# Two graph layers with layer norms: x turned by DMA, the combination product in f16 halves, and a shifted slot table

## The chip, the cores and the metric

The kernel runs on one core of a Trainium2 chip. The metric is the device time of one execution in microseconds (us). Engines are named as in the profile: PE is TensorE's matmuls, PEld its weight loads, DVE is VectorE, ACT ScalarE, POOL GpSimd, SP the engine that issues nearly all DMAs here.

## The reference

```python
# x: (4096, 256), adj: (4096, 4096) int32 with about 0.2% ones
def layer0(x, adj, ...):
    mask = (adj > 0)
    agg = mask @ x / maximum(sum(mask, axis=1), 1.0)
    combined = concatenate([x @ W_self + b_self, agg @ W_nb + b_nb], axis=-1)
    return relu(combined @ W_comb + b_comb)
def layer1(x, neigh, adj, ...):
    neib_att = tanh(neigh @ Wn1 + bn1) @ Wn2 + bn2
    value = neigh @ Wv + bv
    x_att = tanh(x @ Wx1 + bx1) @ Wx2 + bx2
    ws = leaky_relu(x_att @ neib_att.T, 0.01)
    ws = softmax(where(adj > 0, ws, -9e15), axis=1)
    return concatenate([x @ Wfx + bfx, ws @ value], axis=1)
x = layernorm(x + layer0(x, adj, ...))
x = layernorm(x + layer1(x, neigh, adj, ...))
```

## The kernel before

The 4096 rows are worked on in 32 blocks of 128 (`NB`), the 4096 columns of `adj` in 8 groups of 512 (`NG`) for PE and in 4 quarters of 1024 (`NQ`) for masks, exponentials and DMAs. A product that must be exact is made of f16 halves: a "hi" half rounded to f16 and a "lo" half with the rest. The two 256x256 weight products of layer 0 (`W_self` and `W_nb`, each times its half of `W_comb`) are made once, in `m_both`, in f32. x is kept as scaled f16 halves in `x16`.

The order on every engine is written out by slots. Slot s does group s - 8b of block b's aggregation, and whatever else is due: `due(s, at, 0)` is true for block b at slot 8b + at. The constants at the top of the file are these offsets. So eight slots are one block period, and in each slot of the steady part PE does, in this order:

- `turn_p`: four transposes of exponentials into `ps_t`, group k of block b at slot 8b + 32 + k (`TURN_AT`). For an even k it waits for `exp_made`, the exponential of that quarter.
- `aggregate`: eight products of 256 or 257 columns, mask times x.
- the extras that are due: `mean_transpose` (the mean and x turned on PE), `combine` (four f32 products of 256 columns with `m_both`), `x1_transpose`, `hidden_and_fx`, `x_attention`.
- `scores` into `ps_s` (`SCORE_AT`), and `weigh_values`, twelve products into `ps_v` (`WEIGH_AT`), which wait for `p_lo_made`.

ACT does in a slot, in this order: `mean_of`, the copy of the turned mean and x, `normalise1`, `x1_high`, `x_tanh`, `xatt_high`, `exps` (one quarter of a block, in every second slot, from `ROW_MAX_AT` + 1 on), `p_high`, `leaky`, `normalise2`. DVE does `layer1`, `masked_scores`, `x1_low`, `tanh_low`, `row_scale`, `row_max`, `degrees`, `layer0`, `xatt_low` and `add_fx`, `make_mask`, `p_low`. Each engine runs its list strictly in order; semaphores tie the lists together. Two ties matter below. `mean_of` on ACT waits for `degrees` on DVE of the same slot:

```python
def mean_of(b):
    act.wait_ge(degree_step, 2 * (b + 1))
```

and `turn_p` on PE waits for `exps` on ACT of the slot before:

```python
def turn_p(b, k):
    if k % 2 == 0:
        pe.wait_ge(exp_made, NQ * b + k // 2 + 1)
```

The masks are made on DVE, turned by DMA from SP's queue (`turn_mask`) and followed there by the load of the next block's `adj` quarter.

Of the kernel before, what the change touches and what calls it, by code (L numbers as in the profile page):

```python
# [28 lines left out]
X_ONE, X_LO = D, D + 2  # L29
# [29 lines left out]
X1_T_AT = 15  # L59
X1_COPY_AT = 16  # L60
X1_LOW_AT = 17
HIDDEN_AT = 18
TANH_AT = 19
XATT_AT = 20
STACK_AT = 21
SCORE_AT = 22
# [30 lines left out]
def gnn_kernel(nc, x, adj, w_self, b_self, w_nb, b_nb, w_comb, b_comb, neigh, wx1, bx1, wx2, bx2,  # L97
# [5 lines left out]
    with ExitStack() as ctx:  # L103
# [8 lines left out]
        m_both = sb("m_both", [P, DC, 2 * D], F32)  # L112
# [92 lines left out]
        mask_t_in = [sem(f"mask_t_in{q}") for q in range(NQ)]  # L205
        x_in_in = [sem(f"x_in_in{k}") for k in range(2)]
# [41 lines left out]
        mean_x_t_done = sem("mean_x_t_done")  # L248
# [18 lines left out]
        mean_x_t_copied = sem("mean_x_t_copied")  # L267
# [46 lines left out]
        @block.sync  # L314
        def _(sp):
            def load_adj(b, q):
                at_least(sp, mask_made, NQ * (b - 1) + q + 1)
# [36 lines left out]
            for q in range(NQ):
                turn_mask(0, q)
                load_adj(1, q)
            for s in range(0, SLOTS + 3):
                for q, at in enumerate(MASK_SLOTS):
                    if (d := due(s, at, 0)) and d[0] > 0:
                        turn_mask(d[0], q)  # L360
                        if d[0] + 1 < NB:
# [8 lines left out]

        @block.gpsimd
        def _(pool):
# [57 lines left out]
        def _(dve):  # L430
# [94 lines left out]
            def x1_weight_bounds():  # L525
# [5 lines left out]
            def scale_x1_weights():  # L531
# [3 lines left out]
                scale_link(dve.tensor_scalar(w_scale, w_scale, TOP, None, ALU.mult))  # L535
                scale_link(dve.tensor_scalar(x1_inv, w_pow, 1.0 / TOP / X1_SCALE, None, ALU.mult))
# [58 lines left out]
            def first_part(s):  # L595
# [109 lines left out]
            for s in range(0, SLOTS + 3):  # L705
# [27 lines left out]
        def _(act):  # L733
# [61 lines left out]
            def first_part(s):  # L795
# [73 lines left out]
            for s in range(0, SLOTS + 3):  # L869
# [3 lines left out]
                if d := due(s, MEAN_COPY_AT, 0):  # L873
                    mean_x_t_copy(d[0])
# [19 lines left out]
        def _(pe):  # L894
# [89 lines left out]
            def aggregate(b, k):  # L984
# [142 lines left out]
```

## Time and profile before

| | before |
|---|---|
| time, median of 3 runs | 769.79 us (768.95 to 771.76) |
| profiled execution, its own time | 770.73 us |
| its span, first to last instruction | 768.9 us |
| PE busy | 733.2 us, 95% |
| DVE busy | 610.5 us, 79% |
| ACT busy | 584.7 us, 76% |
| granted TensorE clock | 0.996 of full speed |

Matmuls overlap in these records: the time that one costs is the distance to the next one's start, not its own duration. In the same way an ACT or DVE instruction that needs nothing from its predecessor starts before the predecessor's record ends.

### The profile page before, as it was taken

How to read it: one execution, taken by the hardware profiler on the slowest of the kernel's cores; microseconds unless marked ns; L12 is line 12 of the kernel's file. 1: busy time of each engine (PE TensorE's matmuls, PEld its weight loads, DVE VectorE, ACT ScalarE, POOL GpSimd, SP SyncE). 2: the span in 40 equal slices, each digit the busy share in tenths (PEclk: the TensorE clock that was granted, in tenths of full speed). 3: DMA queues.
4: the chain of work that ended last, by engine and by line, in shares of the span. 5: the costliest groups of instructions: out<-in, count | busy, mean ns of one | idle time of the engine just before them, and what ended most of it. 6: DMA issues, size and time to landing. Idle time of an engine off the chain costs nothing.

```text
span 768.9 us, 20264 instructions
## 1 busy us (share of the span) xinstructions
PE 733.2 (95%) x7536; PEld 631.0 (82%) x7536; DVE 610.5 (79%) x1563; ACT 584.7 (76%) x1078; POOL 125.3 (16%) x241
## 2 busy tenths in 40 slices
PE   5989989999999999999999999999999999999785
PEld 4646768888888888888888889888888888887564
DVE  4886477888888888888888888888888888877874
ACT  2455258888888888888888888888888888888995
POOL 0010120111111111111111111111111111111101
PEclk9999999999999999999999999999999999999999
DMA  8968997876677776676876668677667677620000
GB/s 266 363 151 163 220 246 172 179 173 148 157 150 175 176 180 158 158 156 161 180 179 150 160 164 159 167 180 172 138 171 163 170 179 174 122 43 8 8 9 14
DMA packets 175154, 120.43 MB, mean 157 GB/s; under 512 B 140368, under 2 KB 158672, under 8 KB 175056
## 3 DMA queue, kind: packets, MB, share of 16 engines
q1 hardware_dynamic: 174612, 119.11, 65.1%
q8 instruction: 60, 0.98, 0.6%
q14 instruction: 38, 0.31, 0.1%
q10 hardware_dynamic: 444, 0.02, 0.0%
HBM read 81.35 MB, written 4.19 MB: 111 GB/s over the span
## 4 chain that ended last, share of the span: by engine, by line
PE 87%; ACT 4%; DVE 3%; issue 3%; DMA 1%; POOL 1%; SPq 0%; POOLq 0%; ACTq 0%; DVEq 0%
PE ps_v L1036 20%; PE ps_t L1023 14%; PE ps_agg L999 14%; PE ps_agg L1002 14%; PE ps_agg L1056 7%; PE ps_s L1014 6%; PE ps_v L921 2%; PE ps_s L913 2%; PE ps_x L1073 1%; PE ps_x L1076 1%; ACT score L829 1%; DMA neigh_sb<-in_L_gnn_neigh_dram 1%; ACT score L822 1%; PE ps_x L930 1%; PE ps_t L904 1%
## 5 line engine op out<-in xcount | busy, mean ns | idle before, releaser
L999 PE MATMUL ps_agg<-x,mask_t 128*128 128x257 f16 x1024 | 239.7, 272 | 1.5 <-DMA mask_t<-mask 1.5
L1002 PE MATMUL ps_agg<-x,mask_t 128*128 128x256 f16 x1024 | 234.5, 272 | 0.0
L679 DVE TENSOR_TENSOR late<-ps_t,late 128x512 f16<-128x512 f32 x256 | 174.8, 683 | 74.2 <-ACT late L835 71.6
L1036 PEld LDWEIGHTS ps_v<-v,late 128*128 128x128 f16 x3072 | 189.9, 97 | 50.9 <-DVE late L679 16.6
L1036 PE MATMUL ps_v<-v,late 128*128 128x128 f16 x3072 | 213.5, 219 | 9.2 <-DVE late L679 6.7
L822 ACT ACTIVATE score<-ps_s,sc 128x512 f32<-128x512 f32 x256 | 178.0, 695 | 53.0 <-PE ps_s L1014 51.5
L622 DVE CUSTOM_DVE_ANT_0 score<-score,mask 128x512 f32<-128x512 f32 x256 | 176.2, 688 | 18.7 <-ACT score L822 17.2
L835 ACT CAST late<-ps_t 128x512 f16<-128x512 f32 x256 | 150.2, 587 | 15.2 <-PE ps_t L1023 15.1
L1023 PE MATMUL ps_t<-ident,score 128*128 128x128 f32 x1024 | 157.3, 276 | 3.4 <-ACT score L829 3.4
L829 ACT ACTIVATE score<-score,exp_bias,sc 128x1024 f32<-128x1024 f32 x128 | 158.7, 1240 | 1.6 <-DVE exp_bias L631 1.6
L1023 PEld LDWEIGHTS ps_t<-ident,score 128*128 128x128 f32 x1024 | 107.9, 141 | 6.8 <-ACT score L829 4.7
L999 PEld LDWEIGHTS ps_agg<-x,mask_t 128*128 128x128 fp8e4 x1024 | 99.6, 97 | 16.0 <-DMA mask_t<-mask 1.7
L1002 PEld LDWEIGHTS ps_agg<-x,mask_t 128*128 128x128 fp8e4 x1024 | 99.3, 97 | 15.4 <-issue 4.9
L1014 PE MATMUL ps_s<-n,stack 96*128 96x512 f16 x256 | 97.4, 381 | 0.9 <-DVE stack L669 0.9
L486 DVE TENSOR_SCALAR mask<-adj_sb 128x1024 bf16<-128x1024 int32 x128 | 89.6, 702 | 1.1 <-issue 0.2
L415 POOL TENSOR_SCALAR mv<-mv 128x1 f32<-128x1 f32 x32 | 18.9, 591 | 255.5 <-DVE mv L703 255.5
L1056 PE MATMUL ps_agg<-m_both,mean_x_t 128*128 128x256 f32 x256 | 60.5, 379 | 0.0
L812 ACT ACTIVATE mean<-ps_agg,row 128x256 f32<-128x256 f32 x32 | 15.1, 473 | 49.5 <-DVE row L640 49.5
L401 POOL TENSOR_SCALAR mv<-mv 128x1 f32<-128x1 f32 x32 | 8.4, 262 | 261.8 <-DVE mv L653 261.8
L1056 PEld LDWEIGHTS ps_agg<-m_both,mean_x_t 128*128 128x128 f32 x256 | 46.1, 190 | 5.3
L410 POOL TENSOR_TENSOR late<-x,bfv_sb 128x256 f32<-128x256 f32 x32 | 23.8, 745 | 54.2 <-ACT x L841 54.2
L1014 PEld LDWEIGHTS ps_s<-n,stack 96*128 96x128 f16 x256 | 25.0, 98 | 2.9 <-DVE stack L669 1.1
(125 smaller groups left out, 705.7 us busy)
## 6 DMA issues: line engine op xcount, KB each, us to landing
adj_sb<-in_adj_dram SPq DMA_DIRECT2D x128, 512.0 KB, 4.7
neigh_sb<-in_L_gnn_neigh_dram SPq DMA_DIRECT2D x8, 512.0 KB, 8.0
score<-in_x_dram SPq DMA_DIRECT2D x8, 512.0 KB, 8.5
x_in<-in_x_dram SPq DMA_DIRECT2D x32, 128.0 KB, 3.9
out_dram<-out_sb SPq DMA_DIRECT2D x32, 128.0 KB, 4.5
mask_t<-mask SPq DMA_TRANSPOSE x128, 4.2
mask<-in_L_gnn_W_comb_dram SPq DMA_DIRECT2D x1, 512.0 KB, 10.1
mask<-in_L_gnn_W_self_dram SPq DMA_DIRECT2D x1, 256.0 KB, 7.1
```

The costliest lines, as they stand in the source:

```text
L486: dve.tensor_scalar(mask[:, b % MASK_BUFS, q * QW:(q + 1) * QW], adj_sb[:, q, :], 0.0, EDGE, ALU.is_le, ALU.add).then_inc(mask_made, 1)
L622: dve.tensor_tensor_reduce(score[:, b % 2, part], score[:, b % 2, part], mask[:, b % MASK_BUFS, part], 1.0, -3.0e38, ALU.subtract, ALU.max ...
L679: dve.tensor_tensor(p_lo[:, k % 2, :], ps_t[k % 2][:, :], p_hi[:, k % 2, :], ALU.subtract).then_inc(p_lo_made, 1)
L822: act.activation(score[:, b % 2, k * GW:(k + 1) * GW], ps_s[k % 2][:, :], ACT.Prelu, alpha=SLOPE, scale=score_scale).then_inc(leaky_made, 1)
L829: act.activation(part, part, ACT.Exp, bias=exp_bias[:, b % 2:b % 2 + 1], scale=score_unit, accum_out=sums[:, b % 2, q:q + 1]).then_inc(exp ...
L835: act.copy(p_hi[:, k % 2, :], ps_t[k % 2][:, :]).then_inc(p_hi_made, 1)
L999: mm = pe.matmul(agg[:, 0:D + 1], mask_t8[:, c, 0, :], x16[:, c, 0:D + 1], start=(c == 0), stop=(c == NC - 1), skip_group_check=True)
L1002: mm = pe.matmul(agg[:, 0:D], mask_t8[:, c, 0, :], x16[:, c, X_LO:X_LO + D], start=False, stop=False, skip_group_check=True)
L1014: pe.matmul(ps_s[k % 2][:, :], stack[:, b % 2, :], n16[:, k * GW:(k + 1) * GW], start=True, stop=True).then_inc(s_done, 1)
L1023: mm = pe.transpose(ps_t[k % 2][:, u * P:(u + 1) * P], score[:, b % 2, at:at + P], ident[:, :])
L1036: mm = pe.matmul(ps_v[:, 0:DV], p[:, k % 2, chunk], v16[:, c, v:v + DV], start=(c == 0 and part == 0), stop=(c == NC - 1 and part == 2))
L1056: mm = pe.matmul(ps_agg[b % 2][:, 0:D], mean_x_t[:, c * P:(c + 1) * P], m_both[:, dc, half * D:(half + 1) * D], start=(c == 0), stop=(c == ...
```

## The change

x is no longer turned on PE. For each block SP issues one DMA transpose of `x16[:, b]` (both f16 halves, 128x512) into `x_t`. The turned mean is split into f16 halves (`mean_t`), the hi half by ACT (`mean_high`), the lo half by DVE (`mean_low`). `m_both` is scaled and split into `m16` once, during the first slots. `combine` is now twelve f16 products of 256 columns: hi-hi, hi-lo and lo-hi, each over two chunks, for x and for the mean. The result is scaled back in `layer0`'s first operation (`l0_inv`).

```diff
-MASK_SLOTS = (-6, -5, -2, -1)
+MASK_SLOTS = (-7, -5, -1, 0)
 MEAN_AT = 8
 MEAN_T_AT = 9
-MEAN_COPY_AT = 10
-COMBINE_AT = 11
-LAYER0_AT = 12
-X1_AT = 14
+MEAN_SPLIT_AT = 10
+MEAN_LOW_AT = 11
+X_TURN_AT = 4
+COMBINE_AT = 12
+LAYER0_AT = 13
+X1_AT = 15
...
-ROW_MAX_AT = 30
-TURN_AT = 32
-WEIGH_AT = 33
-LAYER1_AT = 41
+ROW_MAX_AT = 31
+TURN_AT = 33
+WEIGH_AT = 34
+LAYER1_AT = 42
...
+            def turn_x(b):
+                sp.wait_ge(x_lo_made, b // TR + 1)
+                at_least(sp, combined, b - 1)
+                sp.dma_start_transpose(x_t[:, b % 2, :, :], x16[:, b, 0:2 * D]).then_inc(x_t_in[b % 2], 16)
...
+            def m_low(c):
+                dve.wait_ge(m_hi_made, c + 1)
+                dve.scalar_tensor_tensor(out=m16[:, 1, c, :], in0=m_both[:, c, :], scalar=m_scale, in1=m16[:, 0, c, :],
+                                         op0=ALU.mult, op1=ALU.subtract).then_inc(m_split, 1)
...
+            def mean_low(b):
+                dve.wait_ge(mean_hi_made, b + 1)
+                dve.scalar_tensor_tensor(out=mean_t[:, 1, :], in0=ps_agg[b % 2][:, 0:D], scalar=x_scale,
+                                         in1=mean_t[:, 0, :], op0=ALU.mult, op1=ALU.subtract).then_inc(mean_lo_made, 1)
...
-            def mean_x_t_copy(b):
-                act.wait_ge(mean_x_t_done, b + 1)
+            def mean_high(b):
+                act.wait_ge(mean_t_done, b + 1)
                 at_least(act, combined, b)
-                act.copy(mean_x_t[:, :], ps_agg[b % 2][:, :]).then_inc(mean_x_t_copied, 1)
+                act.activation(mean_t[:, 0, :], ps_agg[b % 2][:, 0:D], ACT.Copy, scale=x_scale).then_inc(mean_hi_made, 1)
...
             def mean_transpose(b):
                 pe.wait_ge(mean_made, b + 1)
-                pe.wait_ge(x_in_in[b % 2], 16 * (b // 2 + 1))
                 for dc in range(DC):
-                    pe.transpose(ps_agg[b % 2][:, dc * P:(dc + 1) * P], mean[:, dc * P:(dc + 1) * P], ident[:, :])
-                for dc in range(DC):
-                    mm = pe.transpose(ps_agg[b % 2][:, D + dc * P:D + (dc + 1) * P],
-                                      x_in[:, b % 2, dc * P:(dc + 1) * P], ident[:, :])
-                mm.then_inc(mean_x_t_done, 1)
+                    mm = pe.transpose(ps_agg[b % 2][:, dc * P:(dc + 1) * P], mean[:, dc * P:(dc + 1) * P], ident[:, :])
+                mm.then_inc(mean_t_done, 1)
 
             def combine(b):
-                pe.wait_ge(mean_x_t_copied, b + 1)
-                for c in range(2 * DC):
-                    half, dc = divmod(c, DC)
-                    mm = pe.matmul(ps_agg[b % 2][:, 0:D], mean_x_t[:, c * P:(c + 1) * P],
-                                   m_both[:, dc, half * D:(half + 1) * D], start=(c == 0), stop=(c == 2 * DC - 1))
+                if b == 0:
+                    pe.wait_ge(m_split, DC)
+                pe.wait_ge(x_t_in[b % 2], 16 * (b // 2 + 1))
+                pe.wait_ge(mean_lo_made, b + 1)
+                for k, ((r, w), dc) in enumerate(product(HI_LO, range(DC))):
+                    pe.matmul(ps_agg[b % 2][:, 0:D], x_t[:, b % 2, (1 - r) * DC + dc, :], m16[:, w, dc, D:2 * D],
+                              start=(k == 0), stop=False)
+                for k, ((r, w), dc) in enumerate(product(HI_LO, range(DC))):
+                    mm = pe.matmul(ps_agg[b % 2][:, 0:D], mean_t[:, r, dc * P:(dc + 1) * P], m16[:, w, dc, 0:D],
+                                   start=False, stop=(k == 3 * DC - 1))
                 mm.then_inc(combined, 1)
```

All constants between `X1_AT` and `LAYER1_AT` grow by one, so that everything from `combine` on stands one slot later against the aggregation, and the program has one slot more. `MEAN_AT` and `MEAN_T_AT` stay.

On PE, around `combine`, there stood before (`L1056` is `combine`, `L1014` `scores`, `L1036` `weigh_values`, `L1023` `turn_p`, the others `aggregate`):

```order
L999 MATMUL ps_agg<-x,mask_t 128x257
L1056 MATMUL ps_agg<-m_both,mean_x_t 128x256 x4
L1014 MATMUL ps_s<-n,stack 128x512
L1036 MATMUL ps_v<-v,late 128x128 x12
L1023 MATMUL ps_t<-ident,score 128x128 x4
```

and now (`L1097` and `L1100` are `combine`, `L1057` `scores`, `L1079` `weigh_values`, `L1066` `turn_p`):

```order
L1042 MATMUL ps_agg<-x,mask_t 128x257
L1097 MATMUL ps_agg<-m,x_t 128x256 x6
L1100 MATMUL ps_agg<-m,mean_t 128x256 x6
L1057 MATMUL ps_s<-n,stack 128x512
L1079 MATMUL ps_v<-v,late 128x128 x12
L1066 MATMUL ps_t<-ident,score 128x128 x4
```

Four f32 products have become twelve f16 ones; the place within the slot is the same.

On ACT, from the slot 7 places into the block period to the one after it wraps, there stood before (`L841` is `normalise1`, `L835` `p_high`, `L822` `leaky`, `L829` `exps`, `L812` `mean_of`, `L853` `x1_high`):

```order
L841 ACTIVATE x<-l,mv 128x256
L835 CAST late<-ps_t 128x512
L822 ACTIVATE score<-ps_s,sc 128x512
L829 ACTIVATE score,sums<-score,exp_bias,sc 128x1024
L835 CAST late<-ps_t 128x512
L822 ACTIVATE score<-ps_s,sc 128x512
L812 ACTIVATE mean<-ps_agg,row 128x256
L853 ACTIVATE x_t<-ps_x 128x256
L835 CAST late<-ps_t 128x512
L822 ACTIVATE score<-ps_s,sc 128x512
L829 ACTIVATE score,sums<-score,exp_bias,sc 128x1024
```

and now (`L884` is `normalise1`, `L878` `p_high`, `L865` `leaky`, `L855` `mean_of`, `L872` `exps`, `L896` `x1_high`, `L860` `mean_high`):

```order
L884 ACTIVATE x<-l,mv 128x256
L878 CAST late<-ps_t 128x512
L865 ACTIVATE score<-ps_s,sc 128x512
L855 ACTIVATE mean<-ps_agg,row 128x256
L872 ACTIVATE score,sums<-score,exp_bias,sc 128x1024
L878 CAST late<-ps_t 128x512
L865 ACTIVATE score<-ps_s,sc 128x512
L896 ACTIVATE x_t<-ps_x 128x256
L878 CAST late<-ps_t 128x512
L865 ACTIVATE score<-ps_s,sc 128x512
L860 ACTIVATE mean_t<-ps_agg,sc 128x256
```

The first exponential after `normalise1`'s slot now stands behind `mean_of`; before, it stood a slot ahead of it, and `mean_of` had a `p_high` and a `leaky` between itself and the next exponential.

On DVE, at the same place, there stood before (`L622` is `masked_scores`, `L486` `make_mask`, `L679` `p_low`, `L685` to `L689` `row_scale`, `L637` and `L640` `degrees`):

```order
L622 ISA score,part_max<-score,mask 128x512
L622 ISA part_max 128x1
L486 TENSOR_SCALAR mask<-adj_sb 128x1024
L679 TENSOR_TENSOR late<-ps_t,late 128x512
L622 ISA score,part_max<-score,mask 128x512
L622 ISA part_max 128x1
L685 TENSOR_REDUCE row<-sums 128x1
L687 RECIPROCAL row<-row 128x1
L689 TENSOR_SCALAR row<-row,sc 128x1
L637 TENSOR_SCALAR row<-ps_agg,sc 128x1
L640 RECIPROCAL row<-row 128x1
L679 TENSOR_TENSOR late<-ps_t,late 128x512
```

and now (`L659` and `L662` are `row_max`, `L505` `make_mask`, `L717` `p_low`, `L653` `masked_scores`, `L668` and `L671` `degrees`):

```order
L659 TENSOR_REDUCE row<-part_max 128x1
L662 TENSOR_SCALAR exp_bias<-row,sc 128x1
L505 TENSOR_SCALAR mask<-adj_sb 128x1024
L717 TENSOR_TENSOR late<-ps_t,late 128x512
L653 ISA score,part_max<-score,mask 128x512
L653 ISA part_max 128x1
L668 TENSOR_SCALAR row<-ps_agg,sc 128x1
L671 RECIPROCAL row<-row 128x1
L505 TENSOR_SCALAR mask<-adj_sb 128x1024
L717 TENSOR_TENSOR late<-ps_t,late 128x512
```

`row_scale` no longer stands ahead of `degrees`, `row_max` and a mask now stand in the slot before it, and `masked_scores` is still ahead of it.

## Rows read from the trace of the kernel before

**Rows 1.** Windows: first slots, one block period, tail (busy, count, clock, DMA)

```profile
60.00:80.00 20.00, 20.00 (x124) 12.14 (x123) 13.51 (x27) 10.22 (x15) 0.62 (x1) 1.00 0.70 154
400.21:421.10 20.89, 20.89 (x229) 18.67 (x228) 17.48 (x46) 17.13 (x32) 3.75 (x7) 1.00 0.66 165
720.00:740.00 20.00, 16.00 (x183) 12.34 (x183) 16.63 (x49) 18.82 (x36) 2.79 (x5) 1.00 0.02 8
```

**Rows 2.** Waits of PE from 120 to 700 us: the whole answer

```profile
PE ps_t L1023 <- ACT score L829: 0.2, 1, 0.2
```

**Rows 3.** Timeline of PE over one block period: start us, us, instruction

```profile
400.21 0.22 PE L1082 MATMUL ps_x<-tanh,wx 96*96 96x128 f16 x1
...
405.58 0.60 PE L1023 MATMUL ps_t<-ident,score 128*128 128x128 f32 x4
...
408.01 0.61 PE L1023 MATMUL ps_t<-ident,score 128*128 128x128 f32 x4
...
410.22 0.61 PE L1023 MATMUL ps_t<-ident,score 128*128 128x128 f32 x4
...
411.76 0.38 PE L1048 MATMUL ps_agg<-ident,x_in 128*128 128x128 f32 x2
411.98 0.38 PE L1014 MATMUL ps_s<-n,stack 96*128 96x512 f16 x1
412.20 0.83 PE L1036 MATMUL ps_v<-v,late 128*128 128x128 f16 x12
412.92 0.66 PE L1023 MATMUL ps_t<-ident,score 128*128 128x128 f32 x4
413.41 0.27 PE L1002 MATMUL ps_agg<-x,mask_t 128*128 128x256 f16 x1
...
414.29 0.50 PE L1073 MATMUL ps_x<-x_t,wx 128*96 128x128 f16 x6
...
417.17 1.89 PE L1056 MATMUL ps_agg<-m_both,mean_x_t 128*128 128x256 f32 x8
418.89 0.38 PE L1014 MATMUL ps_s<-n,stack 96*128 96x512 f16 x1
...
421.10 0.22 PE L1082 MATMUL ps_x<-tanh,wx 96*96 96x128 f16 x1
```

**Rows 4.** Timeline of ACT around `mean_of`

```profile
405.70 1.23 ACT L829 ACTIVATE score<-score,exp_bias,sc 128x1024 f32<-128x1024 f32 x1
406.83 0.19 ACT L829 ACTIVATION_READ_ACCUMULATOR score<-score,exp_bias,sc 128x1 f32 x1
...
409.83 0.47 ACT L812 ACTIVATE mean<-ps_agg,row 128x256 f32<-128x256 f32 x1 [1.60 <-DVE row L640]
410.21 0.38 ACT L853 ACTIVATE x_t<-ps_x 128x256 f16<-128x256 f32 x1
...
411.51 1.26 ACT L829 ACTIVATE score<-score,exp_bias,sc 128x1024 f32<-128x1024 f32 x1
412.65 0.22 ACT L829 ACTIVATION_READ_ACCUMULATOR score<-score,exp_bias,sc 128x1 f32 x1
```

**Rows 5.** Timeline of DVE around `degrees`

```profile
406.30 0.67 DVE L622 CUSTOM_DVE_ANT_0 score<-score,mask 128x512 f32<-128x512 f32 x1
...
406.90 0.68 DVE L486 TENSOR_SCALAR mask<-adj_sb 128x1024 bf16<-128x1024 int32 x1
...
409.39 0.21 DVE L637 TENSOR_SCALAR row<-ps_agg,sc 128x1 f32<-128x1 f32 x1
409.64 0.16 DVE L640 RECIPROCAL row<-row 128x1 f32<-128x1 f32 x1
```

**Rows 6.** Groups by line, 350 to 518 us: busy us, mean ns

```profile
L657 DVE SCALAR_TENSOR_TENSOR x_t<-ps_x,x_t 128x256 f16<-128x256 f32 x9 | 3.8, 420 | 0.0
L817 ACT COPY mean_x_t<-ps_agg 128x512 f32<-128x512 f32 x9 | 5.6, 617 | 0.0
```

**Rows 7.** DMA issues, 350 to 518 us: median us from issue to landing

```profile
mask_t<-mask SPq DMA_TRANSPOSE x32, 3.8
```

More of the change, by code:

```diff
@@ L28 @@
 XW = 2 * D + 2
-X_ONE, X_LO = D, D + 2
+X_LO, X_HI, X_ONE = 0, D, 2 * D
 EDGE = 1.5 * 2.0 ** -121
@@ L48 @@
 RES_BUFS = 4
-MASK_SLOTS = (-6, -5, -2, -1)
+MASK_SLOTS = (-7, -5, -1, 0)
 MEAN_AT = 8
 MEAN_T_AT = 9
-MEAN_COPY_AT = 10
-COMBINE_AT = 11
-LAYER0_AT = 12
-X1_AT = 14
[L59 to L66, printed above, removed]
-ROW_MAX_AT = 30
-TURN_AT = 32
-WEIGH_AT = 33
-LAYER1_AT = 41
+MEAN_SPLIT_AT = 10
[4 more added lines that the diff above has]
+X1_AT = 15
+X1_T_AT = 16
+X1_COPY_AT = 17
+X1_LOW_AT = 18
+HIDDEN_AT = 19
+TANH_AT = 20
+XATT_AT = 21
+STACK_AT = 22
+SCORE_AT = 23
+ROW_MAX_AT = 31
+TURN_AT = 33
+WEIGH_AT = 34
+LAYER1_AT = 42
 SLOTS = NG * (NB - 1) + LAYER1_AT + 1
@@ L111, in gnn_kernel @@
         neigh_sb = sb("neigh_sb", [P, NB, D], F32)
-        m_both = sb("m_both", [P, DC, 2 * D], F32)
+        m16 = sb("m16", [P, 2, DC, 2 * D], F16)
         v16 = sb("v16", [P, NC, 2 * DV], F16)
@@ L125, in gnn_kernel @@
         bfv_sb = sb("bfv_sb", [P, D], F32)
-        sc = sb("sc", [P, 32], F32)
-        w_top, w_pow, w_scale, x1_inv = sc[:, 24:26], sc[:, 26:28], sc[:, 28:30], sc[:, 30:32]
-        fx_inv, h1_inv = sc[:, 30:31], sc[:, 31:32]
+        sc = sb("sc", [P, 40], F32)
+        w_top, w_pow, w_scale, x1_inv = sc[:, 24:27], sc[:, 27:30], sc[:, 30:33], sc[:, 33:35]
+        m_pow, m_scale, l0_inv = sc[:, 29:30], sc[:, 32:33], sc[:, 35:36]
+        fx_inv, h1_inv = sc[:, 33:34], sc[:, 34:35]
         score_unit, minus_unit, unit_inv = sc[:, 20:21], sc[:, 21:22], sc[:, 22:23]
@@ L146, in gnn_kernel @@
         res = late[:, 1024:2048].rearrange("p (r d) -> p r d", r=RES_BUFS)
+        m_both = late[:, 0:DC * 2 * D].rearrange("p (c d) -> p c d", c=DC)
         x_in = sb("x_in", [P, 2, D], F32)
@@ L149, in gnn_kernel @@
         mean = sb("mean", [P, D], F32)
-        mean_x_t = sb("mean_x_t", [P, 2 * D], F32)
+        mean_t = sb("mean_t", [P, 2, D], F16)
+        x_t = sb("x_t", [P, 2, 2 * DC, P], F16)
         x1 = sb("x1", [P, D], F32)
@@ L205, in gnn_kernel @@
         mask_t_in = [sem(f"mask_t_in{q}") for q in range(NQ)]
+        x_t_in = [sem(f"x_t_in{k}") for k in range(2)]
         x_in_in = [sem(f"x_in_in{k}") for k in range(2)]
@@ L266, in gnn_kernel @@
         mean_made = sem("mean_made")
-        mean_x_t_copied = sem("mean_x_t_copied")
+        mean_hi_made = sem("mean_hi_made")
+        mean_lo_made = sem("mean_lo_made")
+        m_hi_made = sem("m_hi_made")
+        m_split = sem("m_split")
+        m_scaled = sem("m_scaled")
         p_hi_made = sem("p_hi_made")
@@ L362, in _ @@
                             load_adj(d[0] + 1, q)
+                if d := due(s, X_TURN_AT, 0):
+                    turn_x(d[0])
                 if d := due(s, LAYER0_AT + 1, 0):
@@ L475, in x_low @@
                 dve.scalar_tensor_tensor(out=x16[:, part, X_LO:X_LO + D], in0=x_sb[:, part, :], scalar=x_scale,
-                                         in1=x16[:, part, 0:D], op0=ALU.mult, op1=ALU.subtract).then_inc(x_lo_made, 1)
+                                         in1=x16[:, part, X_HI:X_HI + D], op0=ALU.mult, op1=ALU.subtract).then_inc(x_lo_made, 1)
             def make_mask(b, q):
@@ L529, in x1_weight_bounds, with scale_late_weights @@
                                       apply_absolute_value=True).then_inc(w_top_made, 1)
-            def scale_x1_weights():
+                dve.wait_ge(m_copied, DC)
+                dve.tensor_reduce(w_top[:, 2:3], m_both[:, :, :], AX.XY, ALU.max,
+                                  apply_absolute_value=True).then_inc(w_top_made, 1)
+            def scale_late_weights():
                 dve.wait_ge(w_top_reduced, 1)
@@ L534, in scale_x1_weights @@
                 scale_link(dve.reciprocal(w_scale, w_pow))
-                scale_link(dve.tensor_scalar(w_scale, w_scale, TOP, None, ALU.mult))
-                scale_link(dve.tensor_scalar(x1_inv, w_pow, 1.0 / TOP / X1_SCALE, None, ALU.mult))
+                dve.tensor_scalar(w_scale, w_scale, TOP, None, ALU.mult).then_inc(m_scaled, 1)
+                dve.wait_ge(m_scaled, 1)
+                scale_link(dve.tensor_scalar(x1_inv, w_pow[:, 0:2], 1.0 / TOP / X1_SCALE, None, ALU.mult))
+                scale_link(dve.tensor_scalar(l0_inv, x_pow, m_pow, 1.0 / TOP / TOP, ALU.mult, ALU.mult))
             def split_fx():
@@ L606, in first_part @@
                 if s == 3:
-                    x1_weight_bounds()
+                    late_weight_bounds()
                 if s == 5:
-                    scale_x1_weights()
-                if s == 7:
+                    scale_late_weights()
+                if s in (6, 7):
+                    m_low(s - 6)
+                if s == 9:
                     split_fx()
@@ L636, in degrees @@
                 at_least(dve, mean_made, b)
-                dve.tensor_scalar(row[:, 4:5], ps_agg[b % 2][:, X_ONE:X_ONE + 1], EDGE_F8, x_scale, ALU.max,
+                dve.tensor_scalar(row[:, 4:5], ps_agg[b % 2][:, D:D + 1], EDGE_F8, x_scale, ALU.max,
                                   ALU.mult).then_inc(degree_step, 1)
@@ L644, in layer0 @@
                 dve.wait_ge(combined, b + 1)
+                dve.wait_ge(x_in_in[b % 2], 16 * (b // 2 + 1))
                 at_least(dve, x1_made, b)
-                dve.tensor_tensor(l0[:, :], ps_agg[b % 2][:, 0:D], z_bias[:, :], ALU.add).then_inc(l0_step, 1)
+                dve.scalar_tensor_tensor(out=l0[:, :], in0=ps_agg[b % 2][:, 0:D], scalar=l0_inv, in1=z_bias[:, :],
+                                         op0=ALU.mult, op1=ALU.add).then_inc(l0_step, 1)
                 dve.wait_ge(l0_step, base + 1)
@@ L710, in _ @@
                     masked_scores(*d)
+                if d := due(s, MEAN_LOW_AT, 0):
+                    mean_low(d[0])
                 if d := due(s, X1_LOW_AT, 0):
@@ L765, in x_high @@
                 part = slice(TR * i, TR * (i + 1))
-                act.activation(x16[:, part, 0:D], x_sb[:, part, :], ACT.Copy, scale=x_scale).then_inc(x_hi_made, 1)
+                act.activation(x16[:, part, X_HI:X_HI + D], x_sb[:, part, :], ACT.Copy, scale=x_scale).then_inc(x_hi_made, 1)
             act.wait_ge(neigh_w_in, 16 * len(NEIGH_WEIGHTS))
@@ L807, in first_part @@
                     x_high(s + 2)
+                if s in (6, 7):
+                    act.wait_ge(m_scaled, 1)
+                    act.activation(m16[:, 0, s - 6, :], m_both[:, s - 6, :], ACT.Copy, scale=m_scale).then_inc(m_hi_made, 1)
             def mean_of(b):
                 act.wait_ge(degree_step, 2 * (b + 1))
-                at_least(act, mean_x_t_done, b)
+                at_least(act, mean_t_done, b)
                 act.activation(mean[:, :], ps_agg[b % 2][:, 0:D], ACT.Copy, scale=row[:, 5:6]).then_inc(mean_made, 1)
-            def mean_x_t_copy(b):
-                act.wait_ge(mean_x_t_done, b + 1)
+            def mean_high(b):
+                act.wait_ge(mean_t_done, b + 1)
                 at_least(act, combined, b)
-                act.copy(mean_x_t[:, :], ps_agg[b % 2][:, :]).then_inc(mean_x_t_copied, 1)
+                act.activation(mean_t[:, 0, :], ps_agg[b % 2][:, 0:D], ACT.Copy, scale=x_scale).then_inc(mean_hi_made, 1)
             def leaky(b, k):
@@ L872, in _ @@
                     mean_of(d[0])
-                if d := due(s, MEAN_COPY_AT, 0):
-                    mean_x_t_copy(d[0])
+                if d := due(s, MEAN_SPLIT_AT, 0):
+                    mean_high(d[0])
                 if d := due(s, X1_AT, 0):
@@ L998, in aggregate @@
                         if part == "hi":
-                            mm = pe.matmul(agg[:, 0:D + 1], mask_t8[:, c, 0, :], x16[:, c, 0:D + 1], start=(c == 0),
+                            mm = pe.matmul(agg[:, 0:D + 1], mask_t8[:, c, 0, :], x16[:, c, X_HI:X_ONE + 1], start=(c == 0),
                                            stop=(c == NC - 1), skip_group_check=True)
```

8 lines of the change are left out of this document (4 added, 4 removed).

## The prediction

> **What bounds the kernel now.** I read the windows first. In a block period of the steady part PE is busy for all of its 20.89 us, DVE for 17.48, ACT for 17.13, and the DMA engines for 0.66 of it [rows 1]. Then the waits of PE: over 580 us one wait of 0.2 us stands there [rows 2]. So from 120 to 700 us the time is the sum of what PE issues. The tail after the last aggregation is another regime: ACT is busy 18.82 of 20 us there, PE 16.00 [rows 1]. Then the timeline of one period, for the margins behind that full PE. Take the slots modulo 8; I call the slot that starts with `turn_p` at 405.58 slot 7, those at 408.01, 410.22 and 412.92 slots 0, 1 and 2 [rows 3]. A plain slot costs PE 2.21 us (408.01 to 410.22). The exponential that slot 0's `turn_p` needs ends at 406.83 + 0.19 = 407.02 [rows 4], 0.99 us before 408.01 [rows 3]. The one that slot 2's `turn_p` needs ends at 412.65 + 0.22 = 412.87 [rows 4], and the turn starts at 412.92 [rows 3]. The products ahead of it take 2.21 - 0.44 - 0.88 - 0.22 = 0.67 us (0.44 being what a turn takes where PE does not wait, an estimate close to four times 0.11; 8 aggregations 0.88; a score 411.98 to 412.20), so PE was free at 412.87: about 0.05 us of waiting, too short for a row of its own. So this kernel is PE-bound with one place where the margin is nil, and the reader should see what makes it nil: ACT stood idle 1.60 us before `mean_of`, waiting for DVE's `degrees` [rows 4], and DVE reached `degrees` only at 409.39 [rows 5], though the aggregation it reads was complete in slot 7.
>
> **PE's own work.** Removed per block: the f32 products, 417.17 to 418.89, 1.72 us, and x's two transposes, 411.76 to 411.98, 0.22 us [rows 3]. Added: twelve f16 products of 256 columns. Eight of this shape took 413.41 to 414.29, 0.88 us, so 0.11 each [rows 3] and 1.31 for twelve. Net 0.63 us less per block. 31 of 32 combinations stand before the last aggregation, in both versions, and there PE is full: 31 x 0.63 = 19.5 us less. The last one is in the tail, where PE isn't the bound: nothing.
>
> **Small engine work.** ACT's copy of 128x512 (617 ns [rows 6]) becomes one of 128x256, like the 0.38 us of `x1_high` [rows 4]. DVE gains `mean_low`, like the lo half of x1, 420 ns [rows 6]: 17.9 us per period. Both lie under PE. The turned x needs to be there at slot 12 and is asked for at slot 4, eight slots or some 17 us ahead; a mask turn of twice the size lands in 3.8 us [rows 7]. If the cover failed, it would cost at most its landing, under 4 us a block. On SP it stands behind the mask of slot 3 and ahead of the store, and the next mask turn is three slots later. The mask quarters are now made 7, 7, 5 and 6 slots before use instead of 6, 7, 6 and 7: 11 us and more against 3.8. Nothing. The one-time split of `m_both` (a reduce of 128x1024, four operations of 128x512) falls in the first slots, where PE is full for 20 us and DVE works 13.51 of 20 [rows 1]: nothing, with up to 2 us in the range.
>
> By the Trainium skill ("VectorE: DVE Perf Modes", The three transpose paths) a 128x128 transpose takes 1309 ns by DMA and 390 on TensorE, and TensorE is its choice where PSUM will do; here a turn of eight such blocks lands in 3.8 us and two on PE cost 0.22 us, so the trace prices both below the page. By the page's figure the four blocks would take 5.2 us, and if they took all DMA engines, 13.8 + 5.2 = 19.0 of 20.9 us would be filled, near the limit. By the rows it is at most half of 3.8 us, 1.9 us, on top of 0.66 x 20.89 = 13.8 us: 15.7, with room.
>
> **One slot more.** Scores and weighing stand one slot later, so one slot's share of them (2.21 - 0.88 = 1.33 us of PE) leaves the PE-bound part and one slot is added to the tail. There ACT sets the pace (94% busy [rows 1]); its 17.13 us per period are 2.14 a slot, of which I take 2.0, since some small work of the last blocks doesn't come again. Together +0.7 us.
>
> **The new wait.** This decides. `turn_p`, `exps` and `row_max` have moved by a slot, `mean_of` has not. Thus the contents of the old slot 7 now stand in slot 0, together with `degrees` and `mean_of`, and on ACT `mean_of` is directly ahead of the exponential for slot 1's `turn_p`. ACT cannot begin that exponential before DVE has done `degrees`, which is behind `masked_scores`. All the rest up to there (the score, `leaky`, `row_max`, mask, `p_low`, `masked_scores`) is what the old slots 5 to 7 held, in the same order, with the same PE slots beside it, so I put the new instructions into the old slot 7's clock:
>
> - `masked_scores` starts at 406.30, and the next DVE instruction at 406.90 [rows 5]. That is now `degrees`.
> - From the start of `degrees` to that of `mean_of`: 409.39 to 409.83, 0.44 us [rows 4, 5]. `mean_of` at 407.34.
> - `mean_of` to the next ACT instruction: 409.83 to 410.21, 0.38 us [rows 4]. The exponential starts at 407.72, instead of 405.70: 2.02 us late.
> - Exponential to the turn that waits for it: 1.32 us (405.70 to 407.02) to 1.41 (411.51 to 412.92) [rows 3, 4]; 1.39 taken. The turn can start at 409.11.
> - PE is ready for it one slot after 405.58, with `x1_transpose` in it as before: at 408.01 [rows 3].
>
> PE stands still 1.10 us, in every block. Queued behind: the whole of slot 1. No slack of an earlier slot absorbs it, since the chain starts at a score that PE itself issues two slots before. What follows has room: the exponential's 1.23 us from 407.72, then `p_high` (at most the 0.62 of a copy of its size [rows 6]) and `p_low` (taken like the 0.67 of `masked_scores`) end at 410.24, and slot 1's products want them at 409.11 + 0.44 + 0.88 + 0.22 + 0.22 = 410.87, 0.6 us later; in slot 2 the exponential that was just in time before now has no `mean_of` in its chain; its old wait of 0.05 us goes. The combination slot is shorter by 0.42 us, and ACT, which waited in it before, is then just in step.
>
> The wait exists where `mean_of` of block b and the exponential of block b - 3 share a slot: b = 3 to 31, 29 times. 29 x 1.10 = 31.9 us, less 29 x 0.05 = 1.5.
>
> **Sum.** -19.5 + 0.7 + 31.9 - 1.5 = +11.6 us. It is made against the profiled execution (770.73 us, span 768.9), which is 0.9 us above the median of the runs shown, 769.79. On the median: 781.4, say 781.5 us, 1.5% slower.
>
> **Bounds of the wait.** Below: if DVE reached `masked_scores` as soon as `leaky` is done, about 0.5 us earlier than in the old slot 7, the wait would be 0.6 and the sum -3 us. Above: if slot 1 or 2 has a second, smaller wait behind it (the 0.6 us margin for `p_low` used up by clumping on DVE), 0.2 to 0.3 us more a block: +20 us.
>
> **Rivals.**
> - *PE stays full and the kernel is faster.* `mean_of` waits, but the exponential's margin (0.99 us) covers it. It decides if the exponential is less than 1.0 us late instead of 2.02. For it: PE shows no wait now. Against it: the 1.60 us idle before `mean_of` is there already, only with nothing urgent behind. Time: 769.8 - 19.5 - 0.8 = 749.5, or up to 755 with 0.2 us left of the wait.
> - *Gain and wait cancel.* The wait is 0.5 to 0.8 us: 764 to 773.
> - *DMA becomes a bound as well.* The blocks before the scores begin are shorter than 20.9 us and need the same transfers, and every block now adds one. With 0.4 us more a block than my sum: 790 to 797. Against: 15.7 us of DMA in a period of 21.3.
> - *The split's latency.* `mean_high` and `mean_low` don't reach PE by slot 12. They have two slots, some 4 us, for about 0.8 us of work; the time would be as in the case before.
>
> **How the numbers follow.** Forecast (the wait at 0.85 to 1.35 us, 774 to 789) 0.68; PE stays full 0.13; cancel 0.11; DMA or another second wait 0.08. The range takes the forecast, the upper half of the cancelling case and the lower edge of the last: 769 to 791. A measurement can tell this kernel's time to about 0.5%, 3.8 us. Faster: the first rival and a little of the second, 0.15; within 0.5%: 0.10; slower: 0.75.
>
> **What the profile after would show.** Right: PE waits at `turn_p` for ACT's exponential, some 29 times by about 1.1 us, all in slot 1; ACT idles about 1.6 us before `mean_of` with the exponential next; the period is 21.35 us, with the twelve products taking 1.31 in it. PE busy per period falls below it for the first time. Wrong: a period of 20.26 us with PE full (the first rival), waits for `x_t` or `mask_t` (DMA), or for `mean_lo_made`. The prediction fails if DVE runs far enough ahead of its old clock in slot 7, since only there the chain could shrink.

## The result, and the profile after

The changed kernel takes 784.28 us (median of 4 runs, 782.34 to 785.46) against 769.37 us of the kernel before beside it (4 runs, 768.84 to 771.76): ratio 1.0185, 95% interval 1.0155 to 1.0216. It is slower, and the prediction was 781.5.

The profiled execution took 785.46 us with a span of 783.7. First its windows: the first blocks, two short stretches behind them, and one block period (columns as in [rows 1]):

```profile
100.00:113.00 13.00, 10.68 (x91) 8.15 (x90) 10.37 (x30) 7.19 (x15) 1.85 (x3) 1.00 1.17 283
113.00:120.00 7.00, 4.07 (x18) 2.98 (x19) 4.09 (x10) 3.75 (x8) 0.79 (x1) 0.67 0.96 198
116.60:122.20 5.60, 5.60 (x25) 4.39 (x26) 3.03 (x7) 3.26 (x6) 0.00 (x0) 0.50 1.12 276
400.93:422.29 21.36, 20.49 (x233) 18.29 (x230) 17.66 (x48) 17.10 (x34) 3.76 (x8) 1.00 0.77 168
```

The period was 20.89 us with PE full [rows 1]; it is 21.36 with PE busy 20.49. Then the waits of PE from 120 to 700 us, again the whole answer:

```profile
PE ps_t L1066 <- ACT score L872: 23.5, 27, 0.9
```

One wait per block, at `turn_p`, for the exponential: 27 in this window, one before it and one behind it. [rows 2] held 0.2 us. Then PE's timeline around it, slots 7, 0 and 1:

```profile
411.87 0.61 PE L1066 MATMUL ps_t<-ident,score 128*128 128x128 f32 x4
...
414.10 0.61 PE L1066 MATMUL ps_t<-ident,score 128*128 128x128 f32 x4
...
415.87 0.83 PE L1079 MATMUL ps_v<-v,late 128*128 128x128 f16 x12
417.57 0.66 PE L1066 MATMUL ps_t<-ident,score 128*128 128x128 f32 x4 [0.87 <-ACT score L872]
```

The twelve products from 415.87 on need 0.67 us, so PE was free at 416.54 and began at 417.57: 1.03 us. The bracket says 0.87 because matmul records overlap. ACT and DVE over the same stretch (`L855` is `mean_of`, `L872` `exps`, `L653` `masked_scores`, `L668` and `L671` `degrees`, `L717` `p_low`, `L505` `make_mask`):

```profile
406.95 0.69 DVE L717 TENSOR_TENSOR late<-ps_t,late 128x512 f16<-128x512 f32 x1 [1.41 <-ACT late L878]
...
413.49 0.77 DVE L505 TENSOR_SCALAR mask<-adj_sb 128x1024 bf16<-128x1024 int32 x1
414.18 0.68 DVE L717 TENSOR_TENSOR late<-ps_t,late 128x512 f16<-128x512 f32 x1
414.78 0.68 DVE L653 CUSTOM_DVE_ANT_0 score<-score,mask 128x512 f32<-128x512 f32 x1
...
415.38 0.21 DVE L668 TENSOR_SCALAR row<-ps_agg,sc 128x1 f32<-128x1 f32 x1
415.63 0.16 DVE L671 RECIPROCAL row<-row 128x1 f32<-128x1 f32 x1
```

```profile
415.82 0.47 ACT L855 ACTIVATE mean<-ps_agg,row 128x256 f32<-128x256 f32 x1 [1.51 <-DVE row L671]
416.20 1.23 ACT L872 ACTIVATE score<-score,exp_bias,sc 128x1024 f32<-128x1024 f32 x1
417.33 0.19 ACT L872 ACTIVATION_READ_ACCUMULATOR score<-score,exp_bias,sc 128x1 f32 x1
```

Read it from the bottom: the turn at 417.57 waited for the exponential's end at 417.52, the exponential for `mean_of`, `mean_of` for the reciprocal, and that for `masked_scores`. ACT was idle 1.51 us with an exponential behind the instruction that it waited with. In [rows 4] the idle time is nearly the same, 1.60 us, but the exponential had been issued a slot earlier.

Above `masked_scores` the chain goes on along DVE's own queue. `p_low` and a mask stand ahead of it, and DVE had no gap of more than 0.05 us since the `p_low` at 406.95, 7.8 us earlier. So it is DVE's backlog that sets when `degrees` runs, and ACT's order that hands the delay on to PE.

Where the 14.8 us of span come from can be read off the transposes of the mean, one pair per block, which stand in the same slot in both kernels. In the kernel before, those of the first, fifth and last block start at:

```profile
76.44 0.38 PE L1046 MATMUL ps_agg<-ident,mean 128*128 128x128 f32 x2
...
139.99 0.38 PE L1046 MATMUL ps_agg<-ident,mean 128*128 128x128 f32 x2
...
702.80 0.44 PE L1046 MATMUL ps_agg<-ident,mean 128*128 128x128 f32 x2 [0.41 <-ACT mean L812]
```

and in the changed one at:

```profile
75.26 0.38 PE L1088 MATMUL ps_agg<-ident,mean 128*128 128x128 f32 x2
...
141.36 0.38 PE L1088 MATMUL ps_agg<-ident,mean 128*128 128x128 f32 x2
...
716.59 0.38 PE L1088 MATMUL ps_agg<-ident,mean 128*128 128x128 f32 x2
```

So the changed kernel is 1.2 us ahead at the first block and 1.4 us behind at the fifth. It loses 12.4 us in the 27 periods after that (0.46 each), and 1.0 us behind the last mean, where the added slot lies.

### The profile page after: what moved, and what is told of

Its sections match the earlier page's. It is cut to its first block, busy times and chain, and to the rows that moved or that the text cites. A ratio compares the mean times of both kernels' runs of the same rounds, so it can differ in the third digit from the quotient of the medians.

```text
span 783.7 us, 20493 instructions
## 1 busy us (share of the span) xinstructions
PE 723.5 (92%) x7600; PEld 620.5 (79%) x7600; DVE 619.9 (79%) x1599; ACT 584.7 (75%) x1080; POOL 125.2 (16%) x241
## 4 chain that ended last, share of the span: by engine, by line
PE 57%; issue 16%; DVE 12%; ACT 10%; SPq 2%; DMA 1%; POOL 1%; ACTq 0%; POOLq 0%; DVEq 0%
PE ps_v L1079 11%; PE ps_t L1066 10%; PE ps_agg L1042 9%; PE ps_agg L1045 9%; DVE score L653 5%; ACT score L872 5%; PE ps_s L1057 4%; ACT score L865 3%; PE ps_agg L1097 3%; PE ps_agg L1100 3%; PE ps_x L1117 1%; DVE late L717 1%; PE ps_x L1120 1%; SPq L357 1%; PE ps_s L956 1%
## 5 line engine op out<-in xcount | busy, mean ns | idle before, releaser
L717 DVE TENSOR_TENSOR late<-ps_t,late 128x512 f16<-128x512 f32 x256 | 174.7, 682 | 99.7 <-ACT late L878 98.5
L1042 PE MATMUL ps_agg<-x,mask_t 128*128 128x257 f16 x1024 | 244.6, 274 | 0.1
L1045 PE MATMUL ps_agg<-x,mask_t 128*128 128x256 f16 x1024 | 238.7, 274 | 0.3 <-DVE x L494 0.3
L865 ACT ACTIVATE score<-ps_s,sc 128x512 f32<-128x512 f32 x256 | 177.0, 691 | 71.9 <-PE ps_s L1057 71.9
L1079 PEld LDWEIGHTS ps_v<-v,late 128*128 128x128 f16 x3072 | 191.1, 97 | 46.9 <-DVE late L717 16.8
L1079 PE MATMUL ps_v<-v,late 128*128 128x128 f16 x3072 | 213.5, 219 | 9.2 <-DVE late L717 7.0
L1066 PE MATMUL ps_t<-ident,score 128*128 128x128 f32 x1024 | 158.1, 277 | 29.8 <-ACT score L872 29.8
L653 DVE CUSTOM_DVE_ANT_0 score<-score,mask 128x512 f32<-128x512 f32 x256 | 175.5, 686 | 9.6 <-ACT score L865 9.5
L878 ACT CAST late<-ps_t 128x512 f16<-128x512 f32 x256 | 148.5, 580 | 16.0 <-PE ps_t L1066 15.8
L872 ACT ACTIVATE score<-score,exp_bias,sc 128x1024 f32<-128x1024 f32 x128 | 158.0, 1234 | 1.6 <-DVE exp_bias L662 1.6
L1066 PEld LDWEIGHTS ps_t<-ident,score 128*128 128x128 f32 x1024 | 108.5, 141 | 36.4 <-ACT score L872 35.7
L1045 PEld LDWEIGHTS ps_agg<-x,mask_t 128*128 128x128 fp8e4 x1024 | 100.7, 98 | 16.3 <-issue 5.2
L1042 PEld LDWEIGHTS ps_agg<-x,mask_t 128*128 128x128 fp8e4 x1024 | 100.9, 98 | 15.5 <-issue 0.8
L1057 PE MATMUL ps_s<-n,stack 96*128 96x512 f16 x256 | 97.6, 381 | 0.9 <-DVE stack L707 0.9
L505 DVE TENSOR_SCALAR mask<-adj_sb 128x1024 bf16<-128x1024 int32 x128 | 89.5, 702 | 0.3
L855 ACT ACTIVATE mean<-ps_agg,row 128x256 f32<-128x256 f32 x32 | 15.1, 473 | 46.3 <-DVE row L671 46.3
L884 ACT ACTIVATE x<-l,mv 128x256 f32<-128x256 f32 x32 | 19.1, 598 | 11.6 <-POOL mv L424 11.6
L1057 PEld LDWEIGHTS ps_s<-n,stack 96*128 96x128 f16 x256 | 25.0, 98 | 2.7 <-DVE stack L707 1.2
L903 ACT ACTIVATE tanh<-ps_x,bx_sb,sc 96x128 f32<-96x128 f32 x64 | 25.2, 445 | 2.0 <-PE ps_x L1120 2.0
```

The source lines that it names most:

```text
L505: dve.tensor_scalar(mask[:, b % MASK_BUFS, q * QW:(q + 1) * QW], adj_sb[:, q, :], 0.0, EDGE, ALU.is_le, ALU.add).then_inc(mask_made, 1)
L653: dve.tensor_tensor_reduce(score[:, b % 2, part], score[:, b % 2, part], mask[:, b % MASK_BUFS, part], 1.0, -3.0e38, ALU.subtract, ALU.max ...
L717: dve.tensor_tensor(p_lo[:, k % 2, :], ps_t[k % 2][:, :], p_hi[:, k % 2, :], ALU.subtract).then_inc(p_lo_made, 1)
L865: act.activation(score[:, b % 2, k * GW:(k + 1) * GW], ps_s[k % 2][:, :], ACT.Prelu, alpha=SLOPE, scale=score_scale).then_inc(leaky_made, 1)
L872: act.activation(part, part, ACT.Exp, bias=exp_bias[:, b % 2:b % 2 + 1], scale=score_unit, accum_out=sums[:, b % 2, q:q + 1]).then_inc(exp ...
L878: act.copy(p_hi[:, k % 2, :], ps_t[k % 2][:, :]).then_inc(p_hi_made, 1)
```

## The experiments

All times below are medians of 4 or 5 runs. The first four experiments built (`mean_of` last, `degrees` first, the shift alone, the layout alone) ran beside the kernel before at 769.60 us, the other four on another chip beside it at 769.66 us. A period is the mean over the transposes of x1 from the fourth to the thirtieth block.

**mean_of issued last.** On ACT, in the changed kernel:

```diff
-                if d := due(s, MEAN_AT, 0):
-                    mean_of(d[0])
...
                 if d := due(s, SCORE_AT):
                     leaky(*d)
+                if d := due(s, MEAN_AT, 0):
+                    mean_of(d[0])
```

> The changed kernel with one line moved on ACT: mean_of is issued behind leaky of its slot instead of ahead of the exponential. Theory (the wait of TensorE at turn_p is the exponential held up behind mean_of, 1.03 us in each of 29 blocks): the wait goes, the period falls from 21.35 to about 20.35 us, TensorE is full again, time 752 to 757 us. Rival (ACT or DVE are simply overloaded in that slot, or the split and the DMA turn hold TensorE up): the work is the same, so the wait only moves and the time stays within 3 us of 784.

Measured: 750.52 us, ratio 0.9748 (0.9733 to 0.9762). The period in a window, first blocks and one period:

```profile
100.00:125.00 25.00, 21.71 (x201) 17.52 (x199) 20.04 (x55) 17.57 (x34) 2.64 (x4) 1.00 1.14 253
400.00:420.27 20.27, 20.27 (x231) 18.23 (x229) 17.74 (x48) 17.08 (x32) 3.25 (x7) 1.00 0.84 176
```

and ACT at the same place:

```profile
416.29 1.23 ACT L872 ACTIVATE score<-score,exp_bias,sc 128x1024 f32<-128x1024 f32 x1
...
418.72 0.47 ACT L855 ACTIVATE mean<-ps_agg,row 128x256 f32<-128x256 f32 x1
```

PE is full again, the period 1.08 us shorter, and `mean_of` has no wait in front of it at all: the reciprocal that it needs has been done for 0.86 us. DVE's work and its order are the same, so load alone doesn't hold PE up, and the overload rival is out in that form. The time came out 1.5 us below the expected range. The period is 0.08 us shorter than expected, and the first wait fell from 2.83 to 1.14 us, with the granted clock at 1.00 from 100 to 125 us.

**degrees issued first.** On DVE `degrees` is moved ahead of `masked_scores`:

```diff
+                if d := due(s, MEAN_AT, 0):
+                    degrees(d[0])
                 if d := due(s, SCORE_AT + 1):
                     masked_scores(*d)
...
-                if d := due(s, MEAN_AT, 0):
-                    degrees(d[0])
```

> The changed kernel with degrees issued ahead of masked_scores on DVE. Theory (chain p_low, masked_scores, degrees, mean_of, exponential, turn): masked_scores' 0.60 us leave the chain, so the wait shrinks from 1.03 to about 0.43 us and the time by 29 x 0.60 = 17 us to about 767 us. Rival (the slot is overloaded, order does not matter): no change, 784.

Measured: 764.29 us, ratio 0.9926 (0.9912 to 0.9941). The turn in question and its exponential:

```profile
405.48 0.66 PE L1066 MATMUL ps_t<-ident,score 128*128 128x128 f32 x4 [0.26 <-ACT score L872]
```

```profile
403.73 0.47 ACT L855 ACTIVATE mean<-ps_agg,row 128x256 f32<-128x256 f32 x1 [0.90 <-DVE row L671]
404.10 1.23 ACT L872 ACTIVATE score<-score,exp_bias,sc 128x1024 f32<-128x1024 f32 x1
```

ACT's idle time shrank by 0.61 us (1.51 to 0.90) and the period by as much, 21.35 to 20.75. So the wait has the size of the chain: taking 0.6 us out of it gives 0.6 us back. The time is 2.7 us below the expected 767. As with `mean_of` last, the first wait is shorter (1.68 us) and the granted clock stays at 1.00 from 100 to 125 us. By the same reading, the 0.69 us mask in front of `p_low` is another link that could be moved; no run tried that.

**The shift alone.** The kernel before, with `MASK_SLOTS = (-7, -5, -1, 0)` and each of the fifteen constants from `COMBINE_AT` to `LAYER1_AT` one higher:

```diff
-COMBINE_AT = 11
+COMBINE_AT = 12
...
-ROW_MAX_AT = 30
+ROW_MAX_AT = 31
...
-LAYER1_AT = 41
+LAYER1_AT = 42
```

> The kernel before with the shifted slots and the new mask slots alone: f32 combination and transposes of x on TensorE as before. Theory (the shift alone makes the wait, the products alone save): 769.4 + 29 x 1.0 + 0.7 for the slot + 1.5 for the first blocks = about 800 us, a period of about 21.9 us. Rival (the split of the mean or the DMA turn makes the wait): 769 to 772 us.

Measured: 800.11 us, ratio 1.040 (1.038 to 1.042), period 21.92, as expected. Nothing of the split or the DMA turn is in this kernel, and the wait is there (`L812` is `mean_of`, `L829` `exps`, `L640` `degrees`):

```profile
400.71 0.47 ACT L812 ACTIVATE mean<-ps_agg,row 128x256 f32<-128x256 f32 x1 [1.55 <-DVE row L640]
401.09 1.23 ACT L829 ACTIVATE score<-score,exp_bias,sc 128x1024 f32<-128x1024 f32 x1
```

This run moves the masks together with the stages, so it doesn't tell the two apart.

**No shift.** The other part alone: the changed kernel's products, split and DMA turn, `MEAN_LOW_AT = 10`, all other constants and the masks as before.

> The changed kernel's products, split and DMA turn in the slots of the kernel before (combine at 11, mean_low at 10 and all after it as before, masks as before). Theory (the shift alone makes the wait): per block 0.65 us less work, 0.14 more for the aggregation products; but slot 1 is now 0.22 us shorter where slot 2's exponential was just in time, so about 0.2 us of wait stay: 757 to 760 us. Rival (the split needs the shift: combine waits for mean_low): a wait at combine of 0.3 us and more per block, 765 us or above.

Measured: 759.11 us, ratio 0.9859 (0.9844 to 0.9874), period 20.56. `combine` waits for nothing. The 0.2 us left per block are there, though mainly at another instruction than I had said:

```profile
405.30 0.38 PE L1057 MATMUL ps_s<-n,stack 96*128 96x512 f16 x1
405.69 0.83 PE L1079 MATMUL ps_v<-v,late 128*128 128x128 f16 x12
406.42 0.66 PE L1066 MATMUL ps_t<-ident,score 128*128 128x128 f32 x4
```

The products of slot 1 start 0.39 us behind the score instead of 0.22, waiting for `p_low`, which also has `mean_of` in its chain; the turn for the exponential then waits 0.06 more. With the shift alone 30.5 us slower and the rest alone 10.5 us faster, the two add to 20.0, not to the change's 14.9. The difference is about what the 0.23 us of waiting cost over the blocks, some 6 us: they arise only in the old slots. The rest also brings the next point.

**The layout of x16 alone.** In the changed kernel the start of one aggregation product lies on average 111.6 ns behind the one before (some 1,400 pairs from 130 to 690 us), in the kernel before 109.5; the transposes and the products of `weigh_values` are unchanged at 109 and 56 ns, so it isn't the clock. The kernel before with the changed order of columns (the lines that use them follow it):

```diff
-X_ONE, X_LO = D, D + 2
+X_LO, X_HI, X_ONE = 0, D, 2 * D
```

> The kernel before with x16 laid out as in the changed kernel (lo half first, then hi, then the ones) and nothing else. In the changed kernel an aggregation product takes 111.5 ns to the next one instead of 109.6. Theory A (the columns' place in x16 does it): 111.5 ns here too, 64 x 32 x 2 ns = about 4 us slower, 773 to 774. Theory B (the addresses of the buffers behind the enlarged scalar tile, or the extra DMA traffic): 109.6 ns and 769 to 770.

Measured: 772.12 us, ratio 1.0034 (1.0021 to 1.0048), 111.6 ns, period 20.99. The place of the columns does it. The time grew by 2.5 us, less than the 4 us that were expected from the spacing; the period grew by 0.10 us, where 64 products give 0.13. The timeline shows it over eight products, 0.89 us here against 0.88 in [rows 3]:

```profile
405.67 0.27 PE L1002 MATMUL ps_agg<-x,mask_t 128*128 128x256 f16 x1
...
406.56 0.38 PE L1067 MATMUL ps_x<-ident,x 128*128 128x128 f32 x2
```

**Row pitch, and order of the halves.** Both on top of `mean_of` issued last, with one buffer of `x_t` instead of two:

```diff
-XW = 2 * D + 2
+XW = 2 * D + 16
```

> The version with mean_of issued last, x16's row pitch 1056 bytes instead of 1028 (lo, hi, ones in the same order), and one buffer of x_t instead of two to make room. Theory P (the spacing of 111.5 ns comes from where a row begins): back to 109.6 ns or less, 746 to 747 us. Theory D (it comes from the 512 bytes between the halves, or the order of them): 111.5 ns, 750 to 751 us.

```diff
-XW = 2 * D + 2
-X_LO, X_HI, X_ONE = 0, D, 2 * D
+XW = 2 * D + 16
+X_HI, X_ONE, X_LO = 0, D, D + 16
```

> As the run with the pitch of 1056 bytes, but with hi first, the ones behind it and lo 544 bytes after hi; the turn is two DMAs of 128x256. Theory D (order or distance of the halves makes the spacing): 109.6 ns, 746 to 747 us. Theory P (the pitch): the same time as the run with the pitch alone.

Measured: 747.25 us (ratio 0.9706, 0.9691 to 0.9720) and 747.85 us (0.9711, 0.9695 to 0.9727), both with a mean of 109.5 ns and a period of 20.15. With a pitch of 1056 bytes the order no longer matters; with 1028 bytes it does (109.5 with hi first and lo 516 bytes behind it, 111.6 with lo first and hi 512 behind). Theory P holds for the changed kernel, but it is not the pitch alone that is bad. The wider rows also move every buffer allocated behind `x16`, the masks among them, which these two runs don't separate from the pitch. Why one order at 1028 bytes is free stays open. The pitch version is the fastest of all, 2.9% under the kernel before and 3.3 us under the version that it is built on.

**Two DMA turns.** Every turn of x is issued twice, and `combine` waits for both:

```diff
-                sp.dma_start_transpose(x_t[:, b % 2, :, :], x16[:, b, 0:2 * D]).then_inc(x_t_in[b % 2], 16)
+                for again in range(2):
+                    if again:
+                        sp.wait_ge(x_t_in[b % 2], 32 * (b // 2) + 16)
+                    sp.dma_start_transpose(x_t[:, b % 2, :, :], x16[:, b, 0:2 * D]).then_inc(x_t_in[b % 2], 16)
```

> The version with mean_of issued last (750.5 us, TensorE full), with every DMA turn of x issued twice into the same place, the second after the first has landed. Theory (the transfer lies under eight slots): 750 to 752 us, the same period, more only in the first blocks. Rival (the DMA engines or SP's queue are near their bound): waits of TensorE for x_t or mask_t, 5 us or more.

Measured: 757.81 us, ratio 0.9845 (0.9830 to 0.9859): 7.3 us above the version it is built on. The period is 20.27 as there. All of it has arisen by the fourth block. The waits of PE in the first 125 us contain:

```profile
PE ps_agg L1048 <- DMA mask_t<-mask: 5.7, 3, 3.2
PE ps_agg L1045 <- DMA mask_t<-mask: 3.8, 2, 3.1
```

The one of 3.1 us stands at the start of the aggregation, in the version that this run is built on as well:

```profile
48.43 0.28 PE L1042 MATMUL ps_agg<-x,mask_t 128*128 128x257 f16 x1 [3.09 <-DMA mask_t<-mask]
```

The other four, 6.4 us together between 94 and 111 us, are new, and SP's queue shows what the masks stood behind:

```profile
84.23 5.43 SPq L344 DMA_TRANSPOSE x_t<-x  x2
...
100.49 6.13 SPq L344 DMA_TRANSPOSE x_t<-x  x2
```

So my expectation holds for the steady part and fails for the first blocks, and the rival is half right: there a hold of 5 to 6 us on SP can't be absorbed. Whether the transfer or SP's wait between the two is to blame, this run does not separate. A single turn holds SP 1.19 us (the changed kernel's trace), and PE shows no wait for `mask_t` or `x_t` in the changed kernel.

## Why the prediction was right, step by step

- **What bounds it**: right. PE was full, so every microsecond on PE counts, and the first real wait of PE shows in the time.
- **PE's own work**: -0.63 us a block was said. The twelve products took 1.30 us (405.17 to 406.47 in the trace after), the removed ones 1.73 on average and 0.22: -0.65, 20.2 us over 31 blocks.
- **Small work, the DMA turn, the masks**: right in the time; there is no wait for `x_t`, `mask_t` or `mean_lo_made` from 120 to 700 us. Two figures were too low. The DMA share of a period rose from 0.66 to 0.77, 2.7 us, where the bound from the rows was 1.9. The turn of four 128x128 pieces lands in 4.2 us (median, 350 to 518 us), no sooner than that of eight (4.0), where half of 3.8 was taken. The 128x128 price of the Trainium skill ("VectorE: DVE Perf Modes", The three transpose paths), 1309 ns, makes an estimated 5.2 us of these four pieces. The trace doesn't agree: both of its figures are lower.
- **The new wait**: right in place, mechanism and count; 1.03 us against 1.10. `masked_scores` started 0.68 us into slot 0, where I had 0.72, and the links behind it were as read. Above `masked_scores` the reading was less exact: "the chain starts at a score that PE itself issues two slots before" leaves out DVE. `leaky` of that score was done at 414.31, and `masked_scores` started 0.47 us later, out of DVE's backlog. The first of the 29 waits is larger: 2.83 us, where the kernel before had 1.14. The runs with `mean_of` last, `degrees` first and the shift alone show the cause in both directions.
- **What was missed** in the steady part: the layout of `x16`. It costs 2.0 ns in each of 2048 products, 4.1 us by the spacing; the runs that differ by it alone or by the pitch show 2.5 and 3.3 us. I had costed this edit at nothing without naming it. The period closes with it: -0.65 + 1.03 - 0.05 + 0.13 = +0.46 us, as measured.
- **The first blocks** were missed too. PE stood idle for 2.83 us before the turn at 116.59, and the granted clock fell: 1.00 from 100 to 113 us, 0.50 from 116.60 to 122.20, the lower of its two levels (1.2 GHz). PE was full there, and eight aggregation products took 1.71 us against 0.89 in the steady part:

```profile
116.59 1.11 PE L1066 MATMUL ps_t<-ident,score 128*128 128x128 f32 x4 [2.83 <-ACT score L872]
...
117.50 0.42 PE L1045 MATMUL ps_agg<-x,mask_t 128*128 128x256 f16 x1
...
119.21 0.63 PE L1088 MATMUL ps_agg<-ident,mean 128*128 128x128 f32 x2
```

So for 5.6 us PE worked at half speed, which costs 2.8 us there. In the versions with `mean_of` last and `degrees` first, whose first waits are 1.14 and 1.68 us, the clock stays at 1.00. But the run without the shift, whose first wait is 1.14 us as well, has 0.50 from 113.30 to 116.70. So the fall can't be put down to the longer wait alone.

Put together for the profiled executions: work -20.2, layout +4.1, the waits +30.5 (28 of 1.03, and 1.69 more for the first), the old waits -1.5, the added slot +0.7 as forecast, the clock +2.8, the earlier start -1.2. That is +15.2 of the measured +14.8 us; the added slot was not measured by itself. The forecast had +11.6. Its two main terms were right to 0.7 and 1.4 us. The two that it lacked, layout and clock, came to 6.9 us, and the smaller waits, the work and the earlier start took 3.3 of that back. That the total came within 3 us is in part luck.

## What to carry to other kernels

When stages are shifted against each other in a slot table, look at the in-order queues of the small engines: an instruction that waits idly is free only as long as nothing urgent stands behind it, and here moving one line on ACT turned 1.9% slower into 2.5% faster than before. Put the old timestamps under the new order and walk the chain; here the rows of the old trace gave the wait to 0.07 us. And treat a new place of an operand in memory as a change of its own.

## What was not expected of the hardware

The same f16 product of 256 columns costs 109.5 or 111.6 ns depending on how x's halves lie in their row: 1028 bytes a row with hi first and lo 516 bytes on, 109.5; 1028 with lo first and hi 512 on, 111.6; 1056 with either order, 109.5. SP is held nearly as long by a DMA transpose of 128x512 (1.19 us) as by one of 128x1024 (1.23 us), so here a turn of half the size saved the issuing queue nearly nothing. In the first blocks a wait of 2.83 us on PE was followed by 5.6 us at the lower clock, which cost 2.8 us more.
